# VectorE's order in an attention loop: maxima ahead of the normalised outputs, the router's logits a step later, and two reorderings at stage starts

## The reference

```python
def attention(q, k, v):               # 32 query heads, 8 key/value heads, 16 wide
    scores = einsum('bkgsd,bktd->bkgst', qh, kh) / sqrt(16)
    return einsum('bkgst,bktd->bkgsd', softmax(scores), vh)

x = x + tanh(g_xattn) * attention(layernorm(x), ctx, ctx)
h = layernorm(x)
shared = (silu(h @ Wsg) * (h @ Wsu)) @ Wsd * sigmoid(h @ Wse)
probs = softmax(h @ Wr); topw, topi = top_k(probs, 4)      # 32 experts, 64 slots each
# every expert e works on its slots: (silu(xe @ Wg[e]) * (xe @ Wu[e])) @ Wd[e]
x = x + tanh(g_ffn) * (shared + the chosen experts' outputs, weighted)
```

## Time and profile before

| | |
|---|---|
| median of 3 runs | 2271.11 us (2270.77 to 2274.0) |
| the profiled execution's own time | 2271.65 us |
| its span, first to last instruction | 2269.9 us |
| PE busy | 2195.7 us, 97% of the span |
| DVE, ACT, POOL busy | 67%, 52%, 28% |
| mean granted TensorE clock | 0.993 of 2.4 GHz |
| attention stage | about 0 to 706 us |

### The profile page before, as it was taken

One profiled execution on the slowest core, in us unless ns is written; L12 is line 12 of the kernel. 1 busy time (PEld: TensorE's weight loads), 2 busy tenths in 40 slices (PEclk: granted clock), 3 DMA queues, 4 the chain that ended last, 5 costly groups with the idle time before them and its releaser, 6 DMA issues.

```text
span 2269.9 us, 53546 instructions
## 1 busy us (share of the span) xinstructions
PE 2195.7 (97%) x17121; PEld 1846.0 (81%) x17121; DVE 1529.0 (67%) x3139; ACT 1178.3 (52%) x2363; POOL 640.5 (28%) x1488
## 2 busy tenths in 40 slices
PE   6999999999997999999999999999999999999999
PEld 5777777777776888888889888798988989888888
DVE  6999999999996886555556556665555545455554
ACT  5888888888885333334333333433333333333332
POOL 5777777777773100000000003200000100000000
PEclk9999999999998999999999999999999999999999
DMA  3555555555554223442433435424243334344431
GB/s 77 144 143 142 144 142 137 148 143 139 141 151 124 71 72 130 147 150 98 143 126 133 141 122 168 142 84 139 83 141 101 107 102 134 103 154 155 154 103 66
DMA packets 318827, 286.25 MB, mean 126 GB/s; under 512 B 123265, under 2 KB 236929, under 8 KB 318722
## 3 DMA queue, kind: packets, MB, share of 16 engines
q1 hardware_dynamic: 314370, 272.23, 39.2%
q0 software_dynamic: 4352, 12.65, 2.1%
HBM read 195.43 MB, written 88.34 MB: 125 GB/s over the span
## 4 chain that ended last, share of the span: by engine, by line
PE 57%; issue 6%; DMA 3%; DVE 2%; ACT 1%; POOL 0%; DVEq 0%; POOLq 0%; ACTq 0%; SPq 0%
PE p_a L1388 7%; PE acc L1411 6%; PE acc L1412 6%; PE acc L1413 6%; PE p_a L1390 6%; PE p_a L1389 6%; PE p_c L1388 3%; PE p_c L1389 3%; PE p_c L1390 3%; PE p_x L1460 2%; PE p_y L1447 2%; PE p_x L1447 2%; PE p_b L1388 1%; PE p_b L1389 1%; PE p_b L1390 1%
## 5 line engine op out<-in xcount | busy, mean ns | idle before, releaser
L1388 PE MATMUL p_a<-x_h,ws_h 128*128 128x256 f32 x1280 | 377.1, 295 | 16.2 <-ACT term L1124 8.8
L1389 PE MATMUL p_a<-x_l,ws_h 128*128 128x256 f32 x1280 | 363.1, 284 | 0.0
L1390 PE MATMUL p_a<-x_h,ws_l 128*128 128x256 f32 x1280 | 362.9, 284 | 0.0
L1102 ACT ACTIVATE chosen<-chosen 128x256 f32<-128x256 f32 x352 | 146.3, 417 | 394.7 <-DVE chosen L1306 213.5
L589 DVE TENSOR_REDUCE negmax<-p_max 128x8 f32<-128x1024 f32 x256 | 313.1, 1223 | 54.1 <-PE p_max L734 52.7
L1411 PE MATMUL acc<-wd_h,hh 128*128 128x512 f32 x704 | 277.4, 394 | 3.7 <-DVE rows L1326 2.7
L1412 PE MATMUL acc<-wd_l,hh 128*128 128x512 f32 x704 | 275.5, 391 | 0.0
L464 ACT ACTIVATE probs<-p_exp 128x1024 f32<-128x1024 f32 x256 | 261.3, 1021 | 27.2 <-PE p_exp L684 20.5
L1388 PEld LDWEIGHTS p_a<-x_h,ws_h 128*128 128x128 f32 x1280 | 244.9, 191 | 36.9 <-issue 13.6
L1413 PE MATMUL acc<-wd_h,hl 128*128 128x512 f32 x704 | 274.8, 390 | 0.0
L1389 PEld LDWEIGHTS p_a<-x_l,ws_h 128*128 128x128 f32 x1280 | 245.9, 192 | 0.6
(11 more groups left out here) (199 smaller groups left out, 5350.5 us busy)
## 6 DMA issues: line engine op xcount, KB each, us to landing
rows<-out_dram SPq DMA_DIRECT2D x32, 1024.0 KB, 6.3
x_raw<-xn_cols SPq DMA_DIRECT2D x124, 256.0 KB, 2.8
out_dram<-rows SPq DMA_DIRECT2D x31, 1024.0 KB, 4.3
ew<-in_L_ffn_Wg_dram SPq DMA_DIRECT2D x32, 704.0 KB, 6.0
ew<-in_L_ffn_Wu_dram SPq DMA_DIRECT2D x32, 704.0 KB, 7.3
xs<-in_x_dram SPq DMA_DIRECT2D x64, 256.0 KB, 2.7
xres<-in_x_dram SPq DMA_DIRECT2D x64, 256.0 KB, 2.9
out_dram<-x SPq DMA_DIRECT2D x64, 256.0 KB, 2.6
```

Of the source, the lines that this page charges most:

```text
L1102: nc.scalar.activation(act_g[:, cols], gate[:, cols], ACT.Silu).then_inc(silu2_done if half else silu1_done, 1)
L1388: mm(bank, w_h[:, a, k, :], x_h[:, b, k, :], start=start and k == 0, stop=False, skip_group_check=not start)
L1389: mm(bank, w_h[:, a, k, :], x_l[:, b, k, :], start=False, stop=False, skip_group_check=not start)
L1390: last = mm(bank, w_l[:, a, k, :], x_h[:, b, k, :], start=False, stop=(k == 1), skip_group_check=not start)
```

## The change

Four edits.

1. DVE, `body`: the maxima of step 1 stand ahead of the inverted sums, the aggregation and the normalised outputs, no longer behind them. The copy `lg` of the logits stands in step 2 behind the maxima, no longer ahead of the statistics of `x2`.
2. PE, `body`: the logits stand at the end of step 2, behind the turning of the maxima, of the queries and the product `p_max`; before they stood ahead of these.
3. The start: SP issues the first two batches' loads ahead of the four small loads of router weights and gates, and PE and DVE wait for these where they first use them.
4. ACT in the second stage: the key copies come two behind the first copy `term` and two behind the first activation, the exponentials in between.

```diff
@@ SP @@
                     if isinstance(B.n, int) and B.n == 0:
                         load_in(B)
                         load_in(B + 1)
+                        load_weights()
                         load_in(B + 2)
@@ DVE, body @@
                             nc.vector.scalar_tensor_tensor(x2[b.par][:, :], o_sb[:, :], tanh_x[:, 0:1], xres[b.par][:, :],
                                                            ALU.mult, ALU.add).then_inc(x2_done, 1)
-                        if c == 2 and (B - 4).ok:
-                            b = B - 4
-                            dve.wait_ge(lg_mm, b.n + 1)
-                            wait(dve, kept, b.n - 1)
-                            nc.vector.tensor_copy(lg[b.par][:, 0:NE + 1], p_ot[:, 0:NE + 1]).then_inc(lg_done, 1)
-                        if c == 1:
-                            if (B - 2).ok:
-                                inverted = invert_sums(B - 2, 1)
-                            if (B + 2).ok:
-                                aggregate(B + 2, st1, x_stats, mv1, stat1)
-                            if (B - 2).ok:
-                                normalise(B - 2, 1, inverted)
...
                                                     AX.X, ALU.max, negate=True).then_inc(max_done, 1)
+                        if c == 1:
+                            if (B - 2).ok:
+                                inverted = invert_sums(B - 2, 1)
+                            if (B + 2).ok:
+                                aggregate(B + 2, st1, x_stats, mv1, stat1)
+                            if (B - 2).ok:
+                                normalise(B - 2, 1, inverted)
...
+                        if c == 2 and (B - 4).ok:
+                            b = B - 4
+                            dve.wait_ge(lg_mm, b.n + 1)
+                            wait(dve, kept, b.n - 1)
+                            nc.vector.tensor_copy(lg[b.par][:, 0:NE + 1], p_ot[:, 0:NE + 1]).then_inc(lg_done, 1)
@@ PE, body: the block below moves from ahead of L722 in step 2 to behind L734 @@
+                        if c == 2 and (B - 4).ok:
+                            b = B - 4
...
+                            pe.wait_ge(xnT_done, b.n + 1)
+                            pe.wait_ge(ot_done, 2 * b.n + 6 if (b + 2).ok else 2 * NB)
+                            wait(pe, lg_done, b.n)
...
+                            last.then_inc(lg_mm, 1)
@@ ACT, second stage @@
                         nc.scalar.activation(term[:, :], p_a[:, (T.flip + f) % 2, 0:HT], ACT.Copy).then_inc(p1_done, 1)
+                        copy_keys(T, f, (0, 1))
...
                         nc.scalar.activation(sum16, p_a[:, (T.flip + f) % 2, 0:HT], ACT.Copy).then_inc(x16_done, 1)
+                        exponents(T, f)
...
                         silu(T, f, 0)
+                        copy_keys(T, f, (2, 3))
```

More of the change, by code:

```diff
@@ L253, in _, with load_weights @@
             def _(sp):
[L254 to L258, removed]
+                def load_weights():
+                    sp.dma_start(wr[:, :, 0:NE], Wr.rearrange("(k p) e -> p k e", p=128)).then_inc(wr_in, 16)
+                    sp.dma_start(wr[:, :, NE:NE + 1], Wse.rearrange("(k p) e -> p k e", p=128),
+                                 allow_slow_non_contiguous=True).then_inc(wr_in, 16)
+                    sp.dma_start(gx[:, :], g_xattn.rearrange("(a n) -> a n", a=1).to_broadcast([128, 1])).then_inc(g_in, 16)
+                    sp.dma_start(gf[:, :], g_ffn.rearrange("(a n) -> a n", a=1).to_broadcast([128, 1])).then_inc(g_in, 16)
                 def load_in(b):
@@ L512, in _ @@
                 dve.wait_ge(fillers, 2)
-                dve.wait_ge(tanh_done, 2)
                 def stats(source, st):
@@ L564, in body @@
                             b = B - 2
+                            if isinstance(b.n, int) and b.n == 0:
+                                dve.wait_ge(tanh_done, 2)
                             dve.wait_ge(ot_done, 2 * b.n + 2)
@@ L625, in _ @@
                 pe.wait_ge(consts, 1)
-                pe.wait_ge(wr_in, 32)
                 pe.wait_ge(pads, 8)
@@ L699, in body @@
                             pv(B - 1, 0)
[L700 to L710, removed]
                         if c == 0 and (B - 2).ok:
@@ L736, in body @@
                             last.then_inc(p1_mm, 1)
+                        if c == 2 and (B - 4).ok:
+                            b = B - 4
+                            if isinstance(b.n, int) and b.n == 0:
+                                pe.wait_ge(wr_in, 32)
+                            pe.wait_ge(xnT_done, b.n + 1)
+                            pe.wait_ge(ot_done, 2 * b.n + 6 if (b + 2).ok else 2 * NB)
+                            wait(pe, lg_done, b.n)
+                            for k in range(KC):
+                                for j in range(4):
+                                    last = mm(p_ot[32 * j:32 * j + 32, 0:NE + 1], xnT[b.par][:, k, 32 * j:32 * j + 32], wr[:, k, :],
+                                              start=(k == 0), stop=(k == KC - 1))
+                            last.then_inc(lg_mm, 1)
                 iterations(pe, body)
@@ L1109, in high, with copy_keys, exponents @@
                     nc.scalar.activation(hh[:, f, :], act_g, ACT.Copy).then_inc(hh_done, 1)
+                def copy_keys(T, f, qs):
+                    if T.at(0, 0) and f == 0:
+                        act.wait_ge(key_mm, 1)
+                        for q in qs:
+                            bank = (acc[:, 0, :], acc[:, 1, :], p_x[:, :], p_y[:, :])[q]
+                            nc.scalar.activation(keys[:, 512 * q:512 * q + 512], bank, ACT.Copy).then_inc(key_done, 1)
+                def exponents(T, f):
+                    if T.at(0, 0) and f == 0:
+                        act.wait_ge(dv_done, 1)
+                        nc.scalar.activation(route[:, :, TOPK:2 * TOPK], dv[:, :, :], ACT.Exp).then_inc(ew_done, 1)
+                        nc.scalar.activation(ez, zc, ACT.Exp, scale=-1.0).then_inc(ew_done, 1)
                 def body(T, pair, adds):
@@ L1113, in body @@
                         split_x(0, first_block)
[L1114 to L1119, removed]
                     for f in range(T.nf):
```

## The result

The changed kernel takes 2351.55 us in the median (2348.98 to 2352.37, 4 runs), the kernel before 2271.59 us in the same comparison. The ratio is 1.0348, 95% interval 1.0334 to 1.0361: 3.5% slower, about 80 us. Forecast were 2321 us and a range of 2304 to 2336, so the direction was right, the size was not: the loss is 80 us where 50 were forecast.

A forecast was written before the change was run, and what follows sets the result against it. The prediction took two 10.39 us wait cycles between PE and VectorE to bound the kernel. 2271.65 + 54.0 (loop) - 2.06 (start) - 2.35 (second stage) gave 2321 us, range 2304 to 2336.

The forecast's parts named there:

- Loops 1 and 2: Two wait cycles, via maxima 1, L722, o_cols and via maxima 2, p_max of step 3: 10.39 us each; both must shorten.
- The third loop over `lg` and `o_cols`: Attention loop: o_cols of step 3 waits 0.9 to 1.7 us for the late lg, making an iteration 11.44 us.
- The idle time of VectorE ahead of maxima 3: Sign in the attention loop: maxima 3 should show a VectorE wait of over a microsecond.
- The statistics at 5.03 (0.83): VectorE in the loop: statistics start 0.83 us after x2, as before, so 5.03 us after maxima 0.
- ScalarE's share of 2.73 us: PE's stretch from p_max of step 3 to the next step 0 shrinks by 0.03 to 0.04 us, bounds 0 to 0.15.
- 0.76 us from `p_max` to maxima 0: Last step closing each loop: VectorE's maxima start 0.76 us after the p_max they wait for.
- 60 iterations: Iterations having both logits and maxima 2, each growing by 0.90 us: +54.0 us, bounds +42 and +63.
- The start, -2.06: Program start: first token load goes out 2.06 us earlier and all of it arrives; bounds 0 and -2.2.
- The second stage, -2.35: Second stage: ScalarE takes term before the key copies, so PE waits 2.35 us less; from -1.3 to -3.7.
- The late `lg` costs nothing: Rival for the attention loop: o_cols does not lose by lg, iteration 10.57 us, total 2274 us; chance 0.05.
- the earlier maxima pay: Rival for L722 in step 2: earlier maxima 1 shorten the iteration to PE's 10.01 us floor, 2237 us; chance 0.03.
- The clock falls: Rival for PE: standing still about a microsecond each iteration lowers its clock, 84 us more, 2405 us; chance 0.04.

The follow-up runs named there:

- e9: Changed kernel with lg put back ahead of the maxima of step 2 and GpSimd's query subtraction moved behind its copies of the top values: 2272.46 us, ratio 1.0006.
- e3: Changed kernel with lg put back ahead of the maxima of step 2, logits still late on PE: 2301.75 us, ratio 1.0126.
- e5: Changed kernel with the maxima of step 1 put back behind the normalised outputs, lg and logits still late: 2313.68 us, ratio 1.0184.
- e4: Changed kernel with only GpSimd's subtraction for the queries' low parts moved behind its copies of the top values: 2320.63 us, ratio 1.0210.
- e10: Changed kernel with one operand of x2 read from PSUM instead of SBUF, normalisation left out of the residual sum: 2320.38 us, ratio 1.0211.

## Why the prediction was wrong, point by point

- **Loops 1 and 2, and that both must get shorter.** Borne out by e9: maxima 1 came 0.69 us earlier, maxima 2 came 0.25 later, and the period went up by 0.09. The reason given for it was weak. The two sums come out at the same 10.39 because both are the one stretch from 501.30 to 508.20 us, cut at different rows, with the same 2.73 and 0.76 behind it: they would be equal whatever waits for what. In the kernel before, loop 1 does bind in the iteration shown: L722 waits 0.29 us for its maxima. `p_max` of step 3 shows no idle time ahead of it there, and is 1.40 us behind maxima 2 where e9 does it in 1.36; loop 2 was a few hundredths short of binding.
- **The third loop over `lg` and `o_cols`.** Right in mechanism and place, and the wait in size. It was forecast at 0.9 to 1.7 us and is 1.46 in the iteration shown. Removing it gives 50 us (e3); adding it alone costs 42 (2313.68 - 2272.1, e5 against before, with the gain of the two starts in it), or 46.7 in the loop. The idle time of VectorE ahead of maxima 3, named as a sign at over a microsecond, is 0.86 us, and the period is outside the 11.3 to 11.5 us named there.
- **"The statistics at 5.03 (0.83)".** This is the step that failed, a term of the third loop's sum that was too small. It takes the 0.83 us from `x2` to its statistics in the earlier trace rows to hold wherever `x2` stands. Measured is 1.34 (514.27 to 515.61). The sum by its own steps, predicted and measured:

| step | predicted | measured |
|---|---|---|
| maxima 0 to maxima 1 | 2.26 | 2.19 |
| to `rec` | 1.13 | 1.13 |
| to `x2` | 0.81 | 0.90 |
| to the statistics | 0.83 | 1.34 |
| to maxima 2 | 0.65 | 0.61 |
| to `lg` | 1.14 | 1.12 |
| to `o_cols` | 0.34 | 0.33 |
| to `p_max` 3 | 0.79 | 0.82 |
| to `p_max` 0 | 2.73 | 2.64 |
| to maxima 0 | 0.76 | 0.85 |
| sum | 11.44 | 11.93 |

  The sum is 0.49 us longer than calculated; this one step is 0.51 longer, and the others cancel out. e4 and e10, which take it away in two unlike ways, both land at 2320 to 2321 us with a period of 11.39 to 11.40, where the prediction had 2321 and 11.41. That they meet it to 0.02 us is partly luck, since the smaller errors of the table have both signs. The bounds of the range failed for the same reason: they let waits vary and no duration of an instruction that changes its neighbours. The trace of before had the warning in it: the mean of GpSimd's subtraction was 0.957 us over the loop, but 0.70 where it ran at the start of the program, and `x2` itself had 0.75 us in the drain and 0.80 in the loop. I read only VectorE and PE.
- **ScalarE's share of 2.73 us.** Right in sign, 0.09 (2.64); that ScalarE's copies were the reason is not shown.
- **0.76 us from `p_max` to maxima 0.** Too small by 0.09. It was read at maxima 3; maxima 0 start 0.85 to 0.86 us behind their `p_max` in both kernels. In the one before, `p_max` is at 510.93 and VectorE waits for it:

```profile
511.78 1.23 DVE L589 TENSOR_REDUCE negmax<-p_max 128x8 f32<-128x1024 f32 x1 [0.36 <-PE p_max L734]
```

  So most of the 0.12 us between the calculated 10.39 and the measured 10.51, which the prediction put down to VectorE being late at maxima 0, is this term.
- **60 iterations.** Right: 59 give 82.4 us between B = 4 and B = 63, and the 60th wait is there at the beginning of the drain, 1.13 us.
- **The start, -2.06.** Right: the first statistics are at 4.90 instead of 7.08.

```profile
0.75 0.40 SPq L263 DMA_DIRECT2D xs<-in_x_dram  x1
...
4.90 0.69 DVE L518 BATCH_NORM_STATS2 st<-xs 128x6 f32<-128x512 f32 x1
```

- **The second stage, -2.35.** Right: PE's idle time ahead of the second product went from 3.72 to 2.28 us, and what lies behind it was reached 2.4 us sooner after the stage's beginning (790.15 to 797.20, before 707.66 to 717.11). In the profile of the changed kernel the stage began 1.2 us late, which hid half of that. The forecast of 1.4 us of idle time was off, since PE's products just ahead of it had 0.28 us each this time but for the first, at a granted clock of 1.00, where in the kernel before the first seven of the twelve had 0.40 or more, the granted clock being 0.50 until about 712.6 us: PE was through with them about 0.95 us earlier.

```profile
797.20 0.39 PE L1403 MATMUL p_a<-x_h,ws_h 128*128 128x256 f32 x1 [2.28 <-ACT term L1136]
```

- **The rivals.** "The late `lg` costs nothing" is refuted by e5, "the earlier maxima pay" by e9. "The clock falls" is refuted by the window above: 1.00 with a gap of 1.4 us in every iteration, mean 0.996 over the span. The rule of the Trainium skill that I set beside it (page "TensorE: Matmul & The Clock Gate", section "A second HAM failure mode: psum-queue depth-cycling") does not show in this kernel; the measurement decides.

## What to carry to other kernels

Before moving an instruction of VectorE, one that reads two SBUF tensors above all, look at GpSimd's timeline at the old place and at the new one: a duration in a trace can include a wait for the other engine. A small copy that frees a shared bank belongs ahead of the long instruction of its engine, here 0.18 us ahead of 1.2 us, for 50 us in all. And where two loops have nearly the same length, shortening one by a reordering that lengthens the other is a loss, here 5 us; count both before expecting a gain, and take each loop's steps from rows where the wait is seen, since two ways of cutting one stretch of a timeline always add up to the same.

## What the runs showed of the hardware that I had not expected

A VectorE instruction with two SBUF operands (128 x 512, float32) that starts within 0.03 us of a GpSimd subtraction of 0.7 us had 1.28 us instead of 0.75; where it starts 0.21 us ahead of it, GpSimd's two subtractions had 1.87 instead of 1.43 us; with one operand from PSUM neither was longer. One with a single large SBUF operand (`xn`) had 0.86 us instead of 0.54 when another GpSimd subtraction had started 0.2 us ahead of it. PE kept its full granted clock through a gap of 1.4 us in each iteration of 11.9 us.
